# Products of the identity ahead of TensorE's waits in two mixtures' fronts and experts' beginnings

## The chip, the core and the metric

The kernel runs on one core of one Trainium2 chip. The time is that of one execution in microseconds, the median of several runs. The core's engines work side by side and wait for one another by semaphores: TensorE (PE, matrix products), VectorE (DVE), ScalarE (ACT), GpSimd (POOL) and SyncE (SP, which issues DMAs).

## What is computed

Two layers over x of 2 x 1024 tokens by 256, each an attention over a context of 77 rows and a mixture of 8 experts of which every token takes two. The change touches the two mixtures. Cut to them:

```python
def _L0_ffn_ref(hidden_states, router_weight, router_bias, gate_up_proj, gate_up_bias, down_proj, down_bias):
    flat = hidden_states.reshape(B * S, H)
    logits = flat @ router_weight.T + router_bias
    scores = jax.nn.softmax(logits, axis=-1)
    topk_w, topk_idx = jax.lax.top_k(scores, TOP_K)
    gu = jnp.einsum('th,ehn->ten', flat, gate_up_proj) + gate_up_bias
    ...
    down = jnp.einsum('tei,eih->teh', act, down_proj) + down_bias
    gathered = jnp.take_along_axis(down, topk_idx[:, :, None], axis=1)
    out = (gathered * topk_w[:, :, None]).sum(axis=1)

x = x + _L0_xattn_ref(_layernorm(x, axis=-1), ctx_1024, ctx_1024, ...)
x = x + _L0_ffn_ref(_layernorm(x, axis=-1), ...)
x = x + _L1_xattn_ref(ctx_1024, _layernorm(x, axis=-1), ...)
x = x + _L1_ffn_ref(_layernorm(x, axis=-1), ...)
```

The second mixture also normalises the two gates and drops what an expert's capacity doesn't hold. Its hidden width is 1024, the first one's 512.

## The kernel before

The program is a row of blocks. At the end of each, all engines meet, the block's semaphores are cleared, and all go on together. In time: layer 0's attention (to 250 us), mixture 0 (`front` "m0r" from 252, `experts` "m0e" from 290), layer 1's attention (from 525), mixture 1 ("m1r" from 1714, "m1e" from 1752). Each engine runs its own list of instructions in the order written.

**Front** (`front`, line 879). The 2048 tokens are 16 tiles of 128. VectorE normalises a tile (L839, in groups of four), TensorE turns it by two transposes (L956) into one of four PSUM banks, ScalarE copies it out (L988, `xnT`), and TensorE multiplies it with the router (`logits_of`, L947: 128 x 8 columns per product), two tiles behind the transposes. Of each group of four VectorE chooses two experts per token (`choose`, L1011 to L1023); its order is: normalise groups 0 and 1, choose 0, normalise 2, choose 1, normalise 3, choose 2, choose 3. TensorE then waits for all masks (`masks_done`), counts by five bf16 products (L967, L969, `counts_at` lies in the bank of `turned[0]`), and waits for `hot_done`: VectorE meanwhile works out each token's slot by a long chain of small operations and builds one-hot rows in two halves (L1079 to L1083). 16 bf16 products on each half (L974, into `pinv`) invert the list; VectorE turns them into the lists to gather and scatter by (L1092 to L1096). SyncE meanwhile loads up weights, stores the normalised tiles to `xn_rows`, loads the last up weights and a part of the down weights.

**Experts** (`experts`, line 1099). The tokens stand in 39 blocks of 128 rows of one expert. GpSimd gathers rows (L1160), TensorE turns them (`turn_x`, L1182, `pxT`), ScalarE copies them (L1220) and copies the expert's up weights (L1225, `w`), TensorE expands (L1198, 16 products into `ph`), turns the next block, and contracts the block before (L1207, down weights, `py`). At step 1 TensorE waits for `down_ready`: all down weights, whose rest SyncE issues only in this block (L1482, L1471), since their place held the normalised rows until then. Its waits at the beginning are thus: gathered rows, the copies of rows and weights, and, once, the down weights.

fp32 products stand in the trace as two MATMULs each, transposes as one, bf16 products as one.

## Time and profile before

| | us |
|---|---|
| median of 3 runs | 2075.86 (2075.39 to 2076.21) |
| profiled execution | 2081.33 |
| its span | 2079.5 |
| mean granted TensorE clock in it | 0.944 of full |
| TensorE busy | 1897.2 (91%) |
| VectorE busy | 1322.0 (64%) |
| ScalarE busy | 1022.1 (49%) |
| HBM traffic | 50 GB/s over the span |

The profiled execution is 5.5 us above the median. The granted clock is a share of 2.4 GHz, so 0.50 is 1.2 GHz. The page shows it in 40 slices; it is 0.8 or more nearly everywhere, 0.5 in the slices that begin at 260 and 1716 us, and 0.6 and 0.7 in those of 520 and 572. How to read the shares: 91% is a mean of stretches with different limits, and what matters for a change in a front is which wait ends last there.

### The profile page before, as it was taken

How to read it: one execution, taken by the hardware profiler on the slowest of the kernel's cores; microseconds unless marked ns; L12 is line 12 of the kernel's file. 1: busy time of each engine (PE TensorE's matmuls, PEld its weight loads, DVE VectorE, ACT ScalarE, POOL GpSimd, SP SyncE). 2: the span in 40 equal slices, each digit the busy share in tenths (PEclk: the TensorE clock that was granted, in tenths of full speed). 3: DMA queues.
4: the chain of work that ended last, by engine and by line, in shares of the span. 5: the costliest groups of instructions: out<-in, count | busy, mean ns of one | idle time of the engine just before them, and what ended most of it. 6: DMA issues, size and time to landing. Idle time of an engine off the chain costs nothing. (4 is left out here: it accounts for less than half of the span.)

```text
span 2079.5 us, 40140 instructions
## 1 busy us (share of the span) xinstructions
PE 1897.2 (91%) x13658; PEld 1648.1 (79%) x13659; DVE 1322.0 (64%) x2970; ACT 1022.1 (49%) x1761; POOL 608.6 (29%) x542
## 2 busy tenths in 40 slices
PE   6899859999479999999999999999999985999994
PEld 3678759999468888888888888888888865899993
DVE  5445246767657877787787778877777875222223
ACT  3554325554245555555555555555555642444441
POOL 3000003332243432343244324432443200222220
PEclk9999859999679999999999999999999995999997
DMA  6242271111333212320331133213311209111114
GB/s 209 94 145 78 92 285 45 47 48 41 109 72 72 55 39 54 72 53 22 72 72 42 31 73 72 44 32 73 73 35 40 65 2 380 48 36 35 35 35 134
DMA packets 94348, 159.18 MB, mean 77 GB/s; under 512 B 23389, under 2 KB 55513, under 8 KB 92382
## 3 DMA queue, kind: packets, MB, share of 16 engines
q1 hardware_dynamic: 83982, 134.28, 22.7%
q0 software_dynamic: 7888, 20.54, 3.2%
q8 instruction: 101, 1.65, 0.4%
q10 hardware_dynamic: 2304, 2.10, 0.3%
q14 instruction: 73, 0.60, 0.1%
HBM read 71.44 MB, written 32.41 MB: 50 GB/s over the span
## 5 line engine op out<-in xcount | busy, mean ns | idle before, releaser
L1942 ACT ACTIVATE a_prob<-a_slot,a_npeak 128x848 f32<-128x848 f32 x256 | 248.5, 971 | 205.6 <-DVE a_npeak L2003 205.2
L1808 PE MATMUL a_slot<-a_KHL,a_QHL 128*128 128x424 f32 (+1 forms) x1536 | 301.8, 345 | 11.2 <-DVE a_probT L2024 9.3
L2001 DVE TENSOR_REDUCE a_part_peak<-a_slot 128x2 f32<-128x848 f32 x256 | 265.4, 1037 | 37.9 <-PE a_slot L1808 36.8
L1955 ACT ACTIVATE a_probT<-a_slot 128x640 f32<-128x640 f32 x256 | 180.7, 706 | 197.7 <-PE a_slot L1817 153.6
L1833 PE MATMUL a_po<-a_probT,a_V 128*64 128x256 f32 (+1 forms) x2304 | 276.8, 385 | 0.0
L1817 PE MATMUL a_slot<-ident,a_prob 128*128 128x128 f32 x2048 | 268.8, 275 | 0.0
L1808 PEld LDWEIGHTS a_slot<-a_KHL,a_QHL 128*128 128x128 f32 x1536 | 237.9, 191 | 38.5 <-ACT a_probT L1955 13.6
L2033 DVE CUSTOM_DVE_ANT_0 a_masked<-a_prob,a_maskr,a_latent_sum 128x253 f32<-128x253 f32 x256 | 181.8, 710 | 102.5 <-ACT a_prob L1944 87.5
L1817 PEld LDWEIGHTS a_slot<-ident,a_prob 128*128 128x128 f32 x2048 | 236.3, 143 | 8.7 <-issue 0.5
L1833 PEld LDWEIGHTS a_po<-a_probT,a_V 128*64 128x64 f32 (+1 forms) x2304 | 153.8, 136 | 83.3 <-issue 7.3
L1758 PEld LDWEIGHTS a_side<-a_W,a_latT 128*128 128x128 f32 x1536 | 196.6, 199 | 24.1 <-issue 10.8
L1758 PE MATMUL a_side<-a_W,a_latT 128*128 128x128 f32 x1536 | 204.9, 285 | 9.9 <-ACT a_latT L1388 3.8
L2024 DVE COPY a_probT<-a_slot 128x512 f32<-128x512 f32 x256 | 175.2, 685 | 5.2 <-PE a_slot L1817 4.5
L1198 PEld LDWEIGHTS m1e_ph<-m1e_xT,m1e_w 128*128 128x128 f32 x1248 | 147.3, 194 | 8.0 <-ACT m1e_w L1225 3.1
L1198 PE MATMUL m1e_ph<-m1e_xT,m1e_w 128*128 128x128 f32 x1248 | 147.8, 277 | 5.5 <-DMA m_down<-in_L_ffn_W_dram 2.8
L1198 PEld LDWEIGHTS m0e_ph<-m0e_xT,m0e_w 128*128 128x128 f32 x1248 | 147.7, 194 | 6.0 <-ACT m0e_w L1225 3.3
L1198 PE MATMUL m0e_ph<-m0e_xT,m0e_w 128*128 128x128 f32 x1248 | 148.2, 278 | 3.4 <-ACT m0e_w L1225 2.9
L1207 PE MATMUL m1e_py<-m_down,m1e_h 128*128 x624 | 141.0, 379 | 0.0
L1264 DVE TENSOR_TENSOR m1e_h<-m1e_ph,m_bup 128x1024 f32<-128x1024 f32 x39 | 47.8, 1225 | 132.2 <-PE m1e_ph L1198 132.2
L1698 POOL TENSOR_TENSOR a_square<-a_knat 128x1152 f32<-128x1152 f32 x15 | 32.2, 2144 | 336.2 <-ACT a_V L1927 336.2
L1207 PEld LDWEIGHTS m1e_py<-m_down,m1e_h 128*128 128x128 f32 x624 | 115.6, 190 | 14.2
L1944 ACT ACTIVATE a_prob<-a_slot,a_npeak 128x253 f32<-128x253 f32 x256 | 121.1, 473 | 0.0
(321 smaller groups left out, 3021.7 us busy)
## 6 DMA issues: line engine op xcount, KB each, us to landing
a_KHL<-a_KT SPq DMA_DIRECT2D x128, 256.0 KB, 4.4
a_QHL<-a_QT SPq DMA_DIRECT2D x128, 128.0 KB, 2.4
m_up<-_L_ffn_gate_up_proj_dram SPq DMA_DIRECT2D x8, 1024.0 KB, 9.4
m_up<-in_L_ffn_W_dram SPq DMA_DIRECT2D x8, 1024.0 KB, 8.8
m_down<-in_L_ffn_W_dram SPq DMA_DIRECT2D x8, 1024.0 KB, 11.9
a_prob_dram<-a0p_zeros SPq DMA_DIRECT2D x4, 1632.0 KB, 10.7
a_dist_dram<-a_dist SPq DMA_DIRECT2D x4, 1632.0 KB, 5.3
a_band_prob<-a_prob_dram SPq DMA_DIRECT2D x4, 1632.0 KB, 6.9
```

Source lines behind the costliest of these rows:

```text
L1198: ins = nc.tensor.matmul(ph[:, q, cols], w[:, q, c, cols], xT[:, c, :], start=c == 0, stop=c == EC - 1)
L1207: ins = nc.tensor.matmul(py[1 - q][:, 0:E], a[:, 1 - q, f * P:(f + 1) * P], down[:, bass.ds(e, 1), f, :].rearrange("p a n -> p (a n)"), st ...
L1758: ins = t_.matmul(out, x[:, c, :], W[:, parity, i, c, :], start=c == 0, stop=c == EC - 1)
L1808: ins = t_.matmul(out[:, i * BANK:i * BANK + hi - lo], q, KHL[:, pair.parity, h, part, lo:hi], start=part == 0, stop=part == 1)
L1817: ins = t_.transpose(out[:, j * P:(j + 1) * P], prob[:, u % 2, j * P:(j + 1) * P], ident[:, :])
L1833: ins = t_.matmul(po_t[h * D1:(h + 1) * D1, :], V[0:rows, pair.parity, j, h, :], probT[0:rows, gi % 2, j, h, :], start=j == PARTS[0][0], s ...
L1942: a_.activation(prob[:, u % 2, 0:2 * CUT].rearrange("p (n k) -> p n k", n=2), two_banks(slot[u % 2]), ACT.Exp, bias=bias, accum_out=latent ...
L1944: a_.activation(prob[:, u % 2, 2 * CUT:], slot[u % 2][:, 2 * BANK:2 * BANK + REST], ACT.Exp, bias=bias).then_inc(exped, 1)
L1955: a_.activation(probT[:, u // 4 % 2, HALF:KT_TILES, h, u % 2 * P:(u % 2 + 1) * P], slot[u % 2][:, HALF * P:KT_TILES * P].rearrange("p (t q ...
L2001: v.tensor_reduce(part[:, 0:2], two_banks(slot[u % 2]), AX.X, ALU.max).then_inc(part_peaked, 1)
L2024: v.tensor_copy(probT[:, u // 4 % 2, 0:HALF, h, u % 2 * P:(u % 2 + 1) * P], slot[u % 2][:, 0:HALF * P].rearrange("p (t q) -> p t q", q=P)) ...
L2033: v.tensor_tensor_reduce(masked[:, :], prob[:, u % 2, 2 * CUT:], maskr[:, pair.b, :], 1.0, latent_sum[:, u % 2:u % 2 + 1], ALU.mult, ALU.a ...
```

## The change

`keep_clock(nc, out, ident, n)` makes n products of the identity with itself into a place of PSUM that nobody reads. It is called in TensorE's list alone, and it waits for nothing. In each front: 8 ahead of the loop, 1 ahead of each odd tile from the 3rd index on (7 in all), 6 after the last logits, 20 ahead of the wait for the first half of the one-hot rows, and 6 after the last product on them. In each experts' beginning (step 0 only): 16 ahead of the first `turn_x`, 8 after it. To have a place for them, `pinv` becomes a view of a whole bank (`pinv_bank`); the last six of the front go to the bank of `counts_at`, those of the experts to `ph`.

```diff
+def keep_clock(nc, out, ident, n):
+
+    for _ in range(n):
+        nc.tensor.matmul(out, ident[:, :], ident[:, :], start=True, stop=True)
...
-        pinv = ctx.enter_context(nc.psum_tensor(f"{name}_pinv", [P, 3, BLOCKS], F32))
+        pinv_bank = ctx.enter_context(nc.psum_tensor(f"{name}_pinv", [P, BANK], F32))
+        pinv = pinv_bank[:, 0:3 * BLOCKS].rearrange("p (k b) -> p k b", k=3)
...
+            idle = pinv_bank[:, 0:P]
+            keep_clock(nc, idle, ident, 8)
             for t in range(TILES):
+                if t % 2 and t > 2:
+                    keep_clock(nc, idle, ident, 1)
                 pe.wait_ge(dst_done, t + 1)
...
             logits_of(TILES - 1)
+            keep_clock(nc, idle, ident, 6)
             pe.wait_ge(masks_done, TILES // LN_GROUP)
...
                 if k == 0:
+                    if half == 0:
+                        keep_clock(nc, idle, ident, 20)
                     pe.wait_ge(hot_done, half + 1)
...
             ins.then_inc(inverse_done, 1)
+            keep_clock(nc, counts_at[:, 0:P], ident, 6)
...
                 if isinstance(s, int) and s == 0:
+                    keep_clock(nc, ph[:, 0, 0:P], ident, 16)
                     turn_x(0, 0)
+                    keep_clock(nc, ph[:, 0, 0:P], ident, 8)
```

TensorE's list at the start of mixture 0's front, before (L956 transposes, L947 logits; x counts products or transposes of the program):

```order
L67 UNCONDITIONAL_BRANCH
L938 UNCONDITIONAL_BRANCH
L956 MATMUL m0r_turned<-ident,m_down 128x128 x6
L947 MATMUL m0r_pl<-router_Wr,a_latT 128x8 x2
L956 MATMUL m0r_turned<-ident,m_down 128x128 x2
```

The same place now (L845 the added products, L968 transposes, L954 logits):

```order
L945 UNCONDITIONAL_BRANCH
L845 MATMUL m0r_pinv<-ident 128x128 x8
L968 MATMUL m0r_turned<-ident,m_down 128x128 x6
L954 MATMUL m0r_pl<-router_Wr,a_latT 128x8 x2
L845 MATMUL m0r_pinv<-ident 128x128
```

Eight products stand ahead of the first transposes, and then one ahead of every second tile.

TensorE's list from the last logits of the front into the experts, before (L967 and L969 counts, L974 the inversion, L1182 turned rows, L1198 expansion):

```order
L947 MATMUL m0r_pl<-router_Wr,a_latT 128x8 x6
L967 MATMUL m0r_turned<-m0w_M,m0r_ones 128x256
...
L969 MATMUL m0r_pp<-m0w_M,m0r_earlier 128x256
L974 MATMUL m0r_pinv<-m0r_blk1h,m_bdown 128x117 x32
...
L1182 MATMUL m0e_pxT<-ident,m0e_xg 128x128 x2
L1198 MATMUL m0e_ph<-m0e_xT,m0e_w 128x128 x16
```

The same place now:

```order
L845 MATMUL m0r_pinv<-ident 128x128 x6
...
L982 MATMUL m0r_pp<-m0w_M,m0r_earlier 128x256
L845 MATMUL m0r_pinv<-ident 128x128 x20
L989 MATMUL m0r_pinv<-m0r_blk1h,m_bdown 128x117 x32
L845 MATMUL m0r_turned<-ident 128x128 x6
...
L845 MATMUL m0e_ph<-ident 128x128 x16
L1198 MATMUL m0e_pxT<-ident,m0e_xg 128x128 x2
L845 MATMUL m0e_ph<-ident 128x128 x8
L1216 MATMUL m0e_ph<-m0e_xT,m0e_w 128x128 x16
```

Nothing else has moved on TensorE, and the lists of the other engines are the same but for line numbers. Mixture 1 reads alike.

## Rows read from the trace of the kernel before

**Rows 1.** Table of stretches (us, busy per engine, PEclk, DMA share, GB/s)

```profile
255.00:272.00 17.00, 17.00 (x87) 16.93 (x86) 7.84 (x58) 7.26 (x18) 0.00 (x0) 0.50 1.02 397
272.00:283.00 11.00, 1.24 (x6) 0.58 (x5) 9.61 (x40) 0.41 (x2) 0.00 (x0) 0.50 1.05 378
...
300.94:305.80 4.86, 4.86 (x23) 4.86 (x24) 0.00 (x0) 1.75 (x1) 0.00 (x0) 0.50 0.73 257
305.90:307.90 2.00, 1.44 (x13) 1.23 (x13) 0.63 (x1) 0.51 (x2) 0.00 (x0) 1.00 0.00 0
...
1762.61:1766.70 4.09, 4.09 (x19) 4.09 (x20) 0.00 (x0) 1.74 (x1) 0.00 (x0) 0.50 1.08 387
1766.80:1771.40 4.60, 1.84 (x17) 1.61 (x15) 1.22 (x1) 2.69 (x4) 0.00 (x0) 1.00 0.72 256
```

**Rows 2.** TensorE's timeline, mixture 0 (start us, us, what, [idle before, releaser])

```profile
252.76 1.54 PE L956 MATMUL m0r_turned<-ident,m_down 128*128 128x128 f32 x6 [5.74 <-DVE m_down L839]
...
269.46 2.57 PE L947 MATMUL m0r_pl<-router_Wr,a_latT 128*128 128x8 f32 x12
273.87 1.00 PE L967 MATMUL m0r_turned<-m0w_M,m0r_ones 128*128 128x256 bf16 x4 [1.84 <-DVE m0w_M L1023]
...
283.42 1.80 PE L974 MATMUL m0r_pinv<-m0r_blk1h,m_bdown 128*128 128x117 bf16 x16 [8.34 <-DVE m_bdown L1083]
286.41 1.79 PE L974 MATMUL m0r_pinv<-m0r_blk1h,m_bdown 128*128 128x117 bf16 x16 [1.19 <-DVE m_bdown L1083]
297.37 0.69 PE L1182 MATMUL m0e_pxT<-ident,m0e_xg 128*128 128x128 f32 x2 [9.17 <-DMA m0e_xg<-m_xn_rows,m_gather]
300.94 6.18 PE L1198 MATMUL m0e_ph<-m0e_xT,m0e_w 128*128 128x128 f32 x32 [2.88 <-ACT m0e_w L1225]
306.96 0.38 PE L1182 MATMUL m0e_pxT<-ident,m0e_xg 128*128 128x128 f32 x2
```

**Rows 3.** VectorE's timeline, front of mixture 0 and the next block's start

```profile
252.29 2.67 DVE L839 TENSOR_SCALAR m_down<-xres,m0n_moments,m0n_rstd 128x256 f32<-128x256 f32 x8 [3.20 <-PEq L67]
...
258.64 0.19 DVE L1011 TENSOR_TENSOR m0r_logits<-m0r_pl,router_br 128x32 f32<-128x32 f32 x1 [3.22 <-PE m0r_pl L947]
...
260.30 1.38 DVE L839 TENSOR_SCALAR m_down<-xres,m0n_moments,m0n_rstd 128x256 f32<-128x256 f32 x4
263.32 0.19 DVE L1011 TENSOR_TENSOR m0r_logits<-m0r_pl,router_br 128x32 f32<-128x32 f32 x1 [1.64 <-PE m0r_pl L947]
...
272.07 0.19 DVE L1011 TENSOR_TENSOR m0r_logits<-m0r_pl,router_br 128x32 f32<-128x32 f32 x1 [2.30 <-PE m0r_pl L947]
...
288.24 0.20 DVE L1092 COPY m0r_low<-m0r_pinv 128x39 f32<-128x39 f32 x1 [0.77 <-PE m0r_pinv L974]
...
290.25 0.20 DVE L859 TENSOR_TENSOR m0w_free<-m0w_free,m0w_unused 128x39 f32<-128x39 f32 x1 [1.02 <-PEq L67]
```

**Rows 4.** Chain of work that ended last, mixture 1 (start us, us, what)

```profile
1758.81 12.60 DMA m_down<-in_L_ffn_W_dram
...
1778.96 3.57 PE m1e_ph L1198 x32
```

**Rows 5.** TensorE's timeline near the kernel's start, transposes and the next products

```profile
15.51 3.68 PE L154 MATMUL a0ln_turned<-ident,a0p_xn 128*128 128x128 f32 x16 [1.11 <-DVE a0p_xn L134]
20.40 1.29 PE L336 MATMUL a_pk<-a0p_ctxT,a0p_Wk 128*128 128x154 f32 x8 [1.22 <-PEq L67]
```

**Rows 6.** Table of stretches, end of layer 0's attention, columns as in rows 1

```profile
193.00:196.60 3.60, 1.88 (x18) 1.81 (x17) 1.61 (x7) 2.10 (x3) 1.01 (x1) 1.00 0.02 5
196.70:200.00 3.30, 3.30 (x16) 3.12 (x16) 0.00 (x0) 0.98 (x2) 0.00 (x0) 0.50 0.00 0
...
224.00:227.30 3.30, 1.67 (x11) 1.34 (x11) 1.83 (x6) 1.15 (x2) 0.00 (x0) 1.00 0.00 0
...
247.90:252.20 4.30, 0.00 (x0) 0.00 (x0) 1.16 (x7) 0.00 (x0) 1.01 (x1) 0.50 0.00 0
```

**Rows 7.** TensorE's timeline, second expansion of mixture 1

```profile
1771.45 3.84 PE L1198 MATMUL m1e_ph<-m1e_xT,m1e_w 128*128 128x128 f32 x32 [2.81 <-DMA m_down<-in_L_ffn_W_dram]
```

## The prediction

> **What bounds the kernel now.** I read the table of stretches first, since the change lives in four short places of a 2079.5 us span. In the front of mixture 0 TensorE is busy without a break from 255 to 272 us, and the granted clock is 0.50 all that time, as it is after it (272 to 283) and in the experts' first expansion from 300.94 [rows 1]. The front of mixture 1 reads the same. So some 55 us per mixture run at 1.2 GHz instead of 2.4. The TensorE timeline then shows which of that is TensorE's own time: the loop of transposes and logits (252.76 to 272.03), a wait of 1.84 us for the masks, one of 8.34 us for the one-hot rows, 16 + 16 bf16 products with 1.19 us between them, a wait of 9.17 us for the gathered rows, one of 2.88 us for the weights' copy, and 32 expansions in 6.18 us [rows 2]. The VectorE timeline shows who is waited for. VectorE waits for logits at 258.64 (3.22 us), 263.32 (1.64 us) and 272.07 (2.30 us), so TensorE sets the loop; from 272 to 288 VectorE's own chain sets the time, and it waits only 0.77 us for the last bf16 product [rows 3]. Last, the chain of waits: in mixture 1 the second expansion, at 1771.45, is released by a load of the down weights that took 12.60 us to land [rows 4], and the DMA engines are saturated on the way there (1.08 of their time from 1762.61 to 1766.70) [rows 1]. In mixture 0 they are at 0.73 in the stretch that ends at 305.8 and at 0.00 after it [rows 1].
>
> **What one added product costs.** A product of the identity by itself is 128 columns of fp32, as one expansion product, and fp32 expansions stand as two MATMULs in the trace (16 in the order, x32 in the trace). At the high clock 32 of these take 3.57 us [rows 4], or 0.11 each, so 0.22 for a product. At the low clock 16 transposes of 128 columns took 3.68 us [rows 5], 0.23 each, so 0.45 for a product. There are 8 + 7 + 6 + 20 + 6 = 47 in each front and 24 in each experts' beginning.
>
> **Front, the eight ahead.** TensorE enters the block with the others, about when VectorE's first normalisation starts (252.29) [rows 3]. Eight at the low clock are 3.6 us, to 255.85; the first transpose ran at 252.76 [rows 2]. Cost 3.1 us, on the path, since TensorE sets the loop. They can't run at the high clock: TensorE has been idle for 5.7 us by then, and the clock fell within that idle [rows 2, 6].
>
> **When the clock comes up.** In the expansion at 300.94 it was still 0.50 at 305.8 and is 1.00 right after; in that of 1762.61 it is 0.50 to 1766.7 and 1.00 from 1766.8 [rows 1]. So it rose 4.9 and 4.2 us after dense work began. From 252.25 that gives about 256.8: one microsecond into the loop.
>
> **Whether it stays up.** This decides the case. At the high clock a tile of the loop (two transposes, four logit MATMULs) takes about 0.59 us instead of 1.17. But then TensorE runs out of tiles: the third and fourth groups are normalised only after VectorE has chosen for the groups before. The three starts 258.64, 263.32 and 272.07 [rows 3] are 4.68 us apart per group; by my reckoning of the choice (1.7, from 258.64 to the next normalisation at 260.30), normalisation (0.75 to the second tile), two tiles of TensorE and one single product (1.0), latencies (0.3), a group takes 3.7 us at the high clock. In it TensorE streams 8 transposes and 2 products: 8 x 0.11 + 2 x 0.22, about 1.3 us of 3.7, as the logit MATMULs have 8 columns. Nearest rows: the stretch 224.0 to 227.3 has 1.67 us busy of 3.30 and keeps 1.00; that of 193.0 to 196.6 has 1.88 of 3.60, a good part of it in MATMULs of 34 and 51 columns, and the next stretch is at 0.50 [rows 6]. [...] I take it that the clock rises, holds while the first eight tiles are there for the taking, and is lost again when TensorE starts to wait for VectorE.
>
> A rule weighed here: the Trainium skill, "TensorE: Matmul & The Clock Gate", Part 4 (PE-mode transpose), says that the full clock does not engage in transpose mode. This trace speaks against it: after 3.68 us of transposes alone the next product, of 154 columns, ran 8 MATMULs in 1.29 us [rows 5], which is the high pace. By the page the loop would have to live on its single products and the clock would surely be lost; by the row the transposes count, and the case in which it holds keeps a chance.
>
> **The front's sum, clock lost.** Eight ahead: -3.1. Seven singles, five at the low clock (0.45) and two at the high (0.22): -2.7. Some seven tiles at 0.59 instead of 1.17: +4.1. Six after the logits: 2.7 us at the low clock in a wait of 1.84 [rows 2]: -0.9. Twenty: at most 8.9 us in a wait of 8.34, less once the clock rises: 0. Second half of the bf16 products: 1.79 us would be 0.9, and VectorE's wait of 0.77 [rows 3] is all there is to gain; the clock may be either: +0.4. Six at the end: VectorE has 1.0 us left after 288.24 before both meet at the block's end (its idle of 1.02 before 290.25) [rows 3]; they take 1.3 to 2.7: -0.3 to -1.7, taken as -0.6. Sum -2.8 us (the front ends later).
>
> **Experts of mixture 0.** Sixteen (3.6 to 7.2 us) lie in the 7.1 us from the block's start at 290.25 to the gathered rows at 297.37: hidden. Eight (1.8 to 3.6) lie in 2.88 us plus the tail of the transposes: hidden at the high clock. Then the first expansion runs warm: to the next transposes at 306.96 it took 6.02 us, it would take 3.57: +2.45, and the two transposes before it, 0.69, some +0.3. Next in line is the wait for the down weights before the second expansion. DMA is quiet by 305.8 [rows 1]; at -2.8 from the front it is no obstacle. Sum for mixture 0: -2.8 + 2.75, about 0.
>
> **Mixture 1.** The front ends 2.8 us later here too, the first expansion starts at 1765.4 and takes 3.6: 1769.0, with transposes and their copy 1769.9. The down weights come at 1771.45 [rows 4]. Their DMA is issued 2.8 us later, but the engines have a backlog (their share is full, 1.05 in the same place of mixture 0 and 1.08 here [rows 1]), so I leave them there: 0, with a bound of 1 us against. The first expansion's end has 2.81 us of slack today [rows 7]: neither a faster front nor a faster first expansion can gain here. That caps the whole change. Everything after 1771.45, and both long stretches of experts and attention, have the same instructions at a clock of 1.00.
>
> **Forecast.** 2081.33 us of the profiled execution (2079.5 span and 1.8 around it) stand 5.5 above the median of 2075.86; the sum of about 0 applies to both: 2075.9. Own range 2073.5 to 2078.5, from the ends of the last six (1.1), the tiles at the high clock (+/- 2 tiles, 1.2) and 1 us in mixture 1.
>
> **Rivals.**
> 1. The clock holds through the loop. For it: transposes count, and 224 to 227.3 held with half its time idle. Then each front: the first choice starts 1 us late, three group gaps (4.7, 4.7, 4.0) shrink by 1.0, 1.0 and 1.6, so +2.6; the singles are in that; the first six are hidden (1.3 in 1.84); then +0.4 and -1.4, as after twenty products (4.5 of 8.34 us) TensorE idles long enough to lose the clock for the last six: +1.5. Mixture 0: 1.5 + 2.75 = +4.2. In mixture 1 the first expansion would end at about 1764.7, and TensorE would idle 6 us until the down weights; an idle of 5.7 us lost the clock at 252 [rows 6], one of 2.81 kept it [rows 1, 7]. The second expansion then starts low and gives back up to 2.45, say 2.0. Total +2.2: 2073.7; without that loss 2071.7.
> 2. The clock never comes up in the loop (the change doesn't do what it says). The 17 us of unbroken work at 0.50 [rows 1] show that the loop itself doesn't raise it; if eight products are too short a start, the loop runs low with all additions on top: 3.1 + 3.1 + 0.9 + 0.6 + 1.7 = 9.4 per front. Mixture 0: 9.4 - 2.75 = 6.7. Mixture 1: the second expansion at 1762.61 + 9.4 + 3.6 + 0.9 = 1776.5, 5.1 after the down weights. Total 11.8 slower: 2087.7. It turns slower by over 0.2% from some 3 us more than the 2.8 forecast per front, and mixture 1 starts to lose from 4.3 us of delay on. Against it: 3.6 us of products and three tiles' transposes without a gap come close to the 4.2 and 4.9 us after which it rose.
> 3. The forecast with a warm first expansion followed by a lost clock in mixture 1: 2 us more, 2078. It needs TensorE to idle about 4 us or more before 1771.45, so a front that ends no later than now.
>
> **How the numbers follow.** Forecast 0.55, holds 0.27, never comes up 0.08, rival 3 0.10. Measurement tells 0.2% from no change, 4.15 us. Faster: of the holding case the part near 2071.7, and a little for sizes, 0.17. Slower: rival 2 and the upper part of rival 3, 0.12. Within: 0.71. Range 2072.0 to 2079.5, which leaves out rival 2 and the best end of rival 1.
>
> **What would show it.** Right: the clock column reads 0.50, then 1.00 for some 5 to 10 us from about 257, then 0.50 before 272; the third group's choice starts within 1.5 us of today's; the first expansion of both mixtures takes about 3.7 us; the second expansion of mixture 1 is still released by the down weights. Wrong, on the fast side: 1.00 up to the masks and a front shorter by 1.5 us or more; or down weights that land earlier in mixture 1, which I exclude because DMA is saturated. Wrong, on the slow side: 0.50 throughout the loop, or a second expansion of mixture 1 of 5 to 6 us.

## The result, and the profile after

The changed kernel took 2090.86 us in the median of 10 runs (2084.83 to 2099.02), the kernel before 2076.03 in the median of 10 runs beside it (2069.35 to 2084.02). The ratio is 1.0063, with a 95% interval of 1.0046 to 1.0080. That is slower by 13 us, outside the range of 2072.0 to 2079.5 and on the side that had a chance of 0.12.

The traced execution took 2095.3 us, with a span of 2093.5 against 2079.5. Its mean granted clock is **higher** than before, 0.952 against 0.944, and TensorE is busy 40 us longer. Both come with the added products, and neither is time saved. The head of the page after, with the clock row in 40 slices:

```profile
span 2093.5 us, 40708 instructions
...
PE 1937.2 (93%) x13942; PEld 1687.0 (81%) x13943; DVE 1321.6 (63%) x2970; ACT 1021.5 (49%) x1761; POOL 608.3 (29%) x542
...
PEclk9999879999679999999999999999999997999997
```

I cut both traces at four places: SyncE's first DMA issue of a front (the entry), its first issue of the experts (`m_bdown`; from entry to here is "the front"), the start of the second expansion, and its end. All times in us; the start and the end of the second expansion are counted from the entry:

| kernel | mixture | entry | front | 2nd expansion starts | it takes | it ends |
|---|---|---|---|---|---|---|
| before | 0 | 252.24 | 37.96 | 55.66 | 3.81 | 59.47 |
| before | 1 | 1714.18 | 37.97 | 57.27 | 3.84 | 61.11 |
| after | 0 | 256.04 | 41.64 | 57.83 | 3.81 | 61.64 |
| after | 1 | 1721.46 | 42.23 | 61.94 | 5.87 | 67.81 |

The 14.0 us between the two spans are then 3.8 before the first entry, 2.2 in mixture 0, 1.3 from there to mixture 1, and 6.7 in mixture 1. After that both take 304.2. The first and third of these lie in stretches whose instructions are the same, and they are taken up last.

**Front of mixture 0, after.** The TensorE timeline (start, length, engine, line, operation, output<-inputs, count; in brackets the idle time before and who ended it), against [rows 2]. L845 are the added products:

```profile
256.09 3.75 PE L845 MATMUL m0r_pinv<-ident 128*128 128x128 f32 x16 [5.27 <-PEq L67]
259.63 1.49 PE L968 MATMUL m0r_turned<-ident,m_down 128*128 128x128 f32 x6
260.91 0.91 PE L954 MATMUL m0r_pl<-router_Wr,a_latT 128*128 128x8 f32 x4
261.68 0.58 PE L845 MATMUL m0r_pinv<-ident 128*128 128x128 f32 x2
...
277.89 2.91 PE L845 MATMUL m0r_pinv<-ident 128*128 128x128 f32 x12
...
281.62 5.01 PE L845 MATMUL m0r_pinv<-ident 128*128 128x128 f32 x40
290.18 1.80 PE L989 MATMUL m0r_pinv<-m0r_blk1h,m_bdown 128*128 128x117 bf16 x16 [3.55 <-DVE m_bdown L1099]
293.18 1.80 PE L989 MATMUL m0r_pinv<-m0r_blk1h,m_bdown 128*128 128x117 bf16 x16 [1.19 <-DVE m_bdown L1099]
294.77 2.18 PE L845 MATMUL m0r_turned<-ident 128*128 128x128 f32 x12
```

The stretches of the same front (busy time of PE, weight loads, DVE, ACT, POOL; granted clock; DMA share; GB/s), against [rows 1]:

```profile
260.00:262.00 2.00, 2.00 (x12) 1.92 (x11) 0.00 (x0) 1.15 (x3) 0.00 (x0) 0.52 1.02 416
262.00:264.00 2.00, 2.00 (x21) 2.00 (x20) 0.00 (x0) 0.97 (x3) 0.00 (x0) 1.00 1.03 422
264.00:266.00 2.00, 1.84 (x17) 1.75 (x17) 1.42 (x15) 1.98 (x6) 0.00 (x0) 1.00 1.02 412
266.00:268.00 2.00, 1.43 (x14) 1.43 (x15) 1.49 (x5) 1.46 (x4) 0.00 (x0) 1.00 1.06 416
268.00:270.00 2.00, 2.00 (x16) 2.00 (x15) 1.58 (x16) 0.77 (x3) 0.00 (x0) 0.69 1.02 399
270.00:272.00 2.00, 2.00 (x11) 2.00 (x12) 1.32 (x5) 0.70 (x2) 0.00 (x0) 0.50 1.02 403
```

The clock comes up at 261.9, 5.8 us after the eight began, and is lost near 268.8. Against [rows 3], VectorE's choices for the four groups start here:

```profile
264.45 0.19 DVE L1027 TENSOR_TENSOR m0r_logits<-m0r_pl,router_br 128x32 f32<-128x32 f32 x1 [5.22 <-PE m0r_pl L954]
268.28 0.19 DVE L1027 TENSOR_TENSOR m0r_logits<-m0r_pl,router_br 128x32 f32<-128x32 f32 x1 [0.80 <-PE m0r_pl L954]
273.49 0.19 DVE L1027 TENSOR_TENSOR m0r_logits<-m0r_pl,router_br 128x32 f32<-128x32 f32 x1 [2.17 <-PE m0r_pl L954]
278.08 0.19 DVE L1027 TENSOR_TENSOR m0r_logits<-m0r_pl,router_br 128x32 f32<-128x32 f32 x1 [2.84 <-PE m0r_pl L954]
...
297.73 0.20 DVE L865 TENSOR_TENSOR m0w_free<-m0w_free,m0w_unused 128x39 f32<-128x39 f32 x1 [1.73 <-PEq L67]
```

From the entry that is 8.41, 12.24, 17.45 and 22.04, where before had 6.40, 11.08, 15.77 and 19.83. The one gap at the high clock is 3.83; the others are 5.21 and 4.59, longer than before's 4.69 and 4.06.

**Mixture 1, after.** TensorE's second expansion and, below it, the stretches around the block's end at 1763.7. The row of before that answers is [rows 7], with 3.84 us and 2.81 idle:

```profile
1777.48 0.38 PE L1198 MATMUL m1e_pxT<-ident,m1e_xg 128*128 128x128 f32 x2
1783.40 5.87 PE L1216 MATMUL m1e_ph<-m1e_xT,m1e_w 128*128 128x128 f32 x32 [5.53 <-DMA m_down<-in_L_ffn_W_dram]
```

```profile
1758.00:1760.00 2.00, 1.51 (x16) 1.51 (x17) 1.49 (x4) 0.00 (x0) 0.00 (x0) 0.50 1.09 386
1760.00:1762.00 2.00, 2.00 (x12) 2.00 (x11) 0.89 (x5) 0.00 (x0) 0.00 (x0) 0.50 0.56 197
1762.00:1764.00 2.00, 1.22 (x6) 0.95 (x6) 0.26 (x2) 0.00 (x0) 0.00 (x0) 0.50 0.00 0
1764.00:1766.00 2.00, 2.00 (x10) 2.00 (x10) 1.85 (x9) 0.00 (x0) 1.29 (x2) 0.50 0.69 188
```

SyncE's list in the same place (SPq: its issues; the second row is its first issue in the experts):

```profile
1743.91 10.36 SPq L1489 DMA_DIRECT2D m_down<-in_L_ffn_W_dram  x4
1763.69 0.34 SPq L1500 DMA_DIRECT2D m_bdown<-in_L_ffn_b_dram  x1
1764.09 9.77 SPq L1489 DMA_DIRECT2D m_down<-in_L_ffn_W_dram  x4
```

The DMA engines ran dry: their share is 0.56, then 0.00 for the 2 us before 1764. In before they were at work up to the experts' first issue at 1752.15 and beyond it:

```profile
1750.00:1752.00 2.00, 0.16 (x2) 0.00 (x0) 0.89 (x5) 0.00 (x0) 0.00 (x0) 0.50 1.09 385
1752.00:1754.00 2.00, 0.00 (x0) 0.00 (x0) 1.70 (x8) 0.00 (x0) 1.07 (x1) 0.50 1.11 390
```

The later end of the front was therefore passed on to the down weights, which arrived after the first expansion and its transposes had left TensorE idle for 5.53 us. In that idle the clock fell, and the second expansion took 5.87: the clock was at 1.00 up to 59.4 us after the entry and again from 66.2 us on, and the expansion ran from 61.94 to 67.81.

### The profile page after: what moved, and what is told of

Its sections match the earlier page's. It is cut to its first block and busy times, and to the rows that moved or that the text cites. A ratio compares the mean times of both kernels' runs of the same rounds, so it can differ in the third digit from the quotient of the medians.

```text
span 2093.5 us, 40708 instructions
## 1 busy us (share of the span) xinstructions
PE 1937.2 (93%) x13942; PEld 1687.0 (81%) x13943; DVE 1321.6 (63%) x2970; ACT 1021.5 (49%) x1761; POOL 608.3 (29%) x542
```

## The experiments

All edits are against the changed kernel; times of mixture stages are from each one's trace. Kernels in one paragraph's table ran beside before on the same chip.

### One part at a time

`e1_experts_only` takes the five calls out of `front` and keeps the 16 and 8 of the experts:

```diff
-            keep_clock(nc, idle, ident, 8)
...
-                if t % 2 and t > 2:
-                    keep_clock(nc, idle, ident, 1)
...
-            keep_clock(nc, idle, ident, 6)
...
-                    if half == 0:
-                        keep_clock(nc, idle, ident, 20)
...
-            keep_clock(nc, counts_at[:, 0:P], ident, 6)
```

> Only the products of the experts' beginning (16 and 8) are kept, all 47 of each front are left out. From the front's first DMA issue to the first DMA issue of the experts it is 37.97 us before and 41.6 (mixture 0) and 42.2 (mixture 1) with the whole change. Theory A (the cost sits in the longer front and, in mixture 1, in DMA engines that run dry and in a second expansion at the low clock): 38.0 in both mixtures here; mixture 0's second expansion starts 53.0 to 53.6 after the front's first issue instead of 55.66, as the first one runs at the high clock; mixture 1's starts at 57.3 as before, but at the low clock, 5 to 6 us instead of 3.84. In time about -0.5 to the kernel before: 2075.5. Rival B (the products cost something everywhere, in proportion to their number, 48 of 142): +5 us, 2081.

`e2_front_only` is the reverse:

```diff
-                    keep_clock(nc, ph[:, 0, 0:P], ident, 16)
                     turn_x(0, 0)
-                    keep_clock(nc, ph[:, 0, 0:P], ident, 8)
```

> Only the 47 products of each front are kept, the 24 of each experts' beginning are left out. Theory A: fronts of 41.6 and 42.2 us as with the whole change; mixture 0's second expansion 59.3 to 59.8 after the front's first issue (55.66 before, 57.8 with the whole change), since the first one now runs low; mixture 1's second expansion starts at 61.9 as with the whole change, for the down weights, and takes 3.8, as the first one, low and late, leaves TensorE too short an idle to lose the clock. Time +8.5: 2084.5. Rival B: +10 us spread over the kernel, mixture 1's second expansion anywhere.

`e3_no_loop` takes the eight ahead and the singles out:

```diff
-            keep_clock(nc, idle, ident, 8)
...
-                if t % 2 and t > 2:
-                    keep_clock(nc, idle, ident, 1)
```

> The whole change without the eight ahead of the loop and the seven singles. Theory A: the loop is as before (last choice 19.8 us after the front's first issue, 22.0 with the whole change), the six after it cost 0.7, the last six 0.7, so the front takes 39.4 to 39.6; mixture 0's second expansion at 54.4; mixture 1's down weights within 1 us of 57.3, the second expansion low (5 to 6 us). Time +1.3: 2077.3. If the eight and the singles were not what makes the fronts long, these stay near 42 and the time near 2090.

`e4_loop_only` keeps these two and takes all others out:

```diff
-            keep_clock(nc, idle, ident, 6)
...
-                    if half == 0:
-                        keep_clock(nc, idle, ident, 20)
...
-            keep_clock(nc, counts_at[:, 0:P], ident, 6)
...
-                    keep_clock(nc, ph[:, 0, 0:P], ident, 16)
...
-                    keep_clock(nc, ph[:, 0, 0:P], ident, 8)
```

> Only the eight ahead of the loop and the seven singles. Theory A: fronts of 40.2 us (+2.2), the clock up for 7 to 10 us in the loop and then lost; mixture 0's second expansion at 57.9; mixture 1's down weights 1 to 2 us later than 57.3, the second expansion at the high clock, 3.8 us. Time +3.5: 2079.5. If the clock holds here, the front comes below 38.

Beside them before took 2079.86 us. "Stages" is the end of the second expansion from the entry, mixture 0 and 1, against before's 59.47 and 61.11.

| kernel | median | ratio to before (95%) | front 0, 1 | last choice 0, 1 | stages 0, 1 |
|---|---|---|---|---|---|
| e1_experts_only | 2076.47 | 0.9973 (0.9957 to 0.9989) | 37.97, 37.97 | as before | -2.2, +1.7 |
| e2_front_only | 2087.9 | 1.0036 (1.0022 to 1.0051) | 46.73, 41.81 | 26.52, 22.15 | +7.8, +4.8 |
| e3_no_loop | 2079.87 | 1.0000 (0.9981 to 1.0018) | 39.79, 40.06 | as before | +1.1, +4.7 |
| e4_loop_only | 2083.28 | 1.0020 (0.9997 to 1.0042) | 40.77, 40.34 | 22.62, 22.21 | +1.7, +5.3 |

What follows. By the ratios, the experts' part alone is a small gain and the front's part a loss; a cost of the products wherever they stand, the other theory put up for e1 (+5 us), is excluded. In the front, the loop's products cost 2.8 and 2.4 us (e4), and those behind the loop 1.8 and 2.1 (e3).

The ratios and the stages don't agree in size. The two stages together say -0.5 us for e1, +12.6 for e2, +5.8 for e3 and +7.0 for e4; the ratios say -5.6, +7.5, 0 and +4.2. So of e1's gain the stages show 0.5 us. The difference lies outside them: in these four traces the unchanged way from mixture 0 to mixture 1 took 1393.0 to 1396.8 us, against 1402.5 in the trace of before. That spread is taken up last.

Mixture 1 loses in all four, since none brings the down weights earlier. In e4 it also lost the clock, which was not expected: its first expansion ran low (6.79 us), and the second took 5.32 after an idle time of 2.92. In e1 the front is as long as before's, the first expansion is 1.98 us shorter, and TensorE waits the rest and falls to the low clock:

```profile
1750.17 3.84 PE L1209 MATMUL m1e_ph<-m1e_xT,m1e_w 128*128 128x128 f32 x32 [0.89 <-ACT m1e_w L1236]
...
1759.33 5.31 PE L1209 MATMUL m1e_ph<-m1e_xT,m1e_w 128*128 128x128 f32 x32 [5.11 <-DMA m_down<-in_L_ffn_W_dram]
```

One front went another way. In mixture 0 of e2 the eight products took as long as in the others (3.75 us from 246.92), but the clock stayed low through the whole loop, the last choice was 6.7 us late, and the front was 8.8 us longer than before's. This is the prediction's rival 2 (9.4 per front), in one front:

```profile
253.00:256.00 3.00, 3.00 (x17) 3.00 (x16) 0.00 (x0) 0.97 (x3) 0.00 (x0) 0.50 1.04 421
256.00:259.00 3.00, 3.00 (x16) 3.00 (x15) 1.50 (x15) 1.80 (x4) 0.00 (x0) 0.50 1.01 403
...
266.00:270.00 4.00, 4.00 (x21) 4.00 (x21) 1.21 (x14) 1.15 (x3) 0.00 (x0) 0.50 1.10 379
```

### Does a longer front reach the down weights?

`e10_end_only` has no added product but 12 at the end of each front, where they do nothing except lengthen it:

```diff
-            keep_clock(nc, counts_at[:, 0:P], ident, 6)
+            keep_clock(nc, counts_at[:, 0:P], ident, 12)
```

> The kernel before with 12 products after the front's last bf16 product and nothing else: it lengthens the front alone, behind all of its work. At the low clock 12 take 5.4 us, of which 1.0 lies beside VectorE: front 42.2 us instead of 37.97. Theory A (mixture 1's down weights come late because the front is longer: the DMA engines run dry before the rest of the loads is issued): mixture 1's second expansion starts at 61.5 to 62 us after the front's first issue, as with the whole change (61.94), with a stretch of 2 to 3 us of idle DMA before the experts' first issue. Rival C (the down weights come late for something else that the products do, such as TensorE's reading beside the DMA's writing in the experts): 57.3 to 58.5, since TensorE makes nothing there.

Mixture 1's front took 40.91, 2.94 longer (42.2 in all was expected; the clock came up within the 12); its second expansion started at 60.30, 3.03 later; one execution took 2093.07. The DMA engines run out in the same way (stretches of e10, whose experts' first issue is at 1764.32; below them TensorE's second expansion):

```profile
1762.00:1764.00 2.00, 1.58 (x13) 1.39 (x11) 0.00 (x0) 0.00 (x0) 0.00 (x0) 0.92 0.58 204
1764.00:1766.00 2.00, 0.00 (x0) 0.00 (x0) 1.53 (x7) 0.00 (x0) 0.98 (x1) 0.93 0.35 123
...
1783.71 3.84 PE L1208 MATMUL m1e_ph<-m1e_xT,m1e_w 128*128 128x128 f32 x32 [2.79 <-DMA m_down<-in_L_ffn_W_dram]
```

So the delay passes one for one. Over all kernels with the loads as they were, the second expansion starts 18.9 to 21.1 us after the experts' first issue: 19.30 to 19.87 in three traces of before, 18.92 to 19.71 in four of the changed kernel, 19.39 in e10. The backlog of DMA was worth less than 2 us: with the issue moved back, the front's own loads are through 39.6 us after the entry (the share of 0.56 in the changed kernel, of 0.58 here), and before issues at 37.97, 1.6 us ahead of that. Even these 1.6 us can't be seen in the landings. e10 makes the delay alone: its second expansion kept the clock.

`e5_early_down` lets SyncE issue all four late loads of down weights in the front, before it waits for the block's end:

```diff
+            sp.wait_ge(logits_done, TILES)
+            load_weights(sp, 2)
...
+                if stage == 2:
+                    load_down(sp, range(NE - lent, NE))
...
-                load_down(sp, range(NE - lent, NE))
```

> The whole change, and the rest of the down weights is loaded in the front, as soon as the normalised rows are stored and the last logits are made (their place is free then), instead of in the experts. The front keeps its length. Theory A: no idle DMA in mixture 1, its second expansion starts at 57.3 to 58.5 after the front's first issue instead of 61.94, still at the low clock; mixture 0's stays at 57.8. Time -4 us to the changed kernel. Rival C: 61 to 62 as before it.

2083.38 us, ratio 1.0018 (1.0002 to 1.0034), beside a before of 2078.66. The second expansion no longer waits for DMA, but mixture 1's front grew to 46.23. SyncE is held by its own issues, and everyone waits for it at the block's end (SyncE, then TensorE, whose idle time now lies there):

```profile
1743.14 22.55 SPq L1491 DMA_DIRECT2D m_down<-in_L_ffn_W_dram  x8
1766.57 1.69 SPq L1504 DMA_DIRECT2D m_bdown<-in_L_ffn_b_dram  x1
...
1766.62 6.54 PE L845 MATMUL m1e_ph<-ident 128*128 128x128 f32 x32 [4.30 <-PEq L67]
...
1781.12 3.81 PE L1218 MATMUL m1e_ph<-m1e_xT,m1e_w 128*128 128x128 f32 x32 [0.56 <-ACT m1e_xT L1240]
```

`e12_two_early` issues two of the four there, in mixture 1 alone:

```diff
+                if stage == 2 and layer == 1:
+                    load_down(sp, range(NE - lent, NE - lent + 2))
...
-                load_down(sp, range(NE - lent, NE))
+                load_down(sp, range(NE - lent + 2 * layer, NE))
```

> The whole change, and in mixture 1 two of the four late down weight loads are issued in the front, once the last logits are made, so that SyncE is done with them at about 39 us, ahead of the front's own end. Theory A: the front stays at 42.2, the DMA engines stay full up to its end, the second expansion of mixture 1 starts at 57.5 to 59.5 instead of 61.94, still low. Rival C: 61 to 62.

2085.14 us, 1.0018 (0.9999 to 1.0036), beside a before of 2078.42. Here SyncE is free in time (front 42.62, against 42.23 in the changed kernel), and the second expansion starts at 57.66 instead of 61.94, released by ScalarE's copy and not by a load, and takes 3.81:

```profile
1743.23 15.84 SPq L1491 DMA_DIRECT2D m_down<-in_L_ffn_W_dram  x6
1763.35 0.34 SPq L1504 DMA_DIRECT2D m_bdown<-in_L_ffn_b_dram  x1
1763.74 3.69 SPq L1491 DMA_DIRECT2D m_down<-in_L_ffn_W_dram  x2
...
1778.39 3.81 PE L1218 MATMUL m1e_ph<-m1e_xT,m1e_w 128*128 128x128 f32 x32 [0.57 <-ACT m1e_xT L1240]
```

That takes 6.3 of mixture 1's 6.7 us away. The late issue of the down weights is the cause of that part, shown from both sides: e10 makes the delay, e12 takes it away and with it the idle time in which the clock fell.

### Keeping the clock in the wait for the down weights

`e6_step1_filled` adds products ahead of that wait in mixture 1:

```diff
+                    keep_clock(nc, ph[:, 1, 0:P], ident, 24 if layer == 1 else 0)
```

> The whole change with 24 products more in mixture 1, between the first expansion and the wait for the down weights (5.53 us of idle in the changed kernel, after which the second expansion took 5.87). 24 at the high clock take 5.35 us. Theory A: the second expansion of mixture 1 starts where it did, at 61.9 after the front's first issue, and takes 3.8 us: -2.0 us there. If the products delay more than they give back, the second expansion starts later than the down weights land and is no longer released by DMA.

The second expansion took 3.84 instead of 5.87, so the low pace came from the idle time. It began at 63.29, not at the 61.9 expected, as the weights landed later in this trace, 21.07 after the first issue; one execution took 2089.79, which says no more than that.

`e8_experts_early_filled` is e1, e5 and e6 together:

> A version meant to beat both: no product in the fronts, 16 and 8 in the experts' beginnings, 24 ahead of the wait for the down weights in mixture 1, and the rest of the down weights loaded in the front. Theory A: fronts of 38.0; mixture 0's second expansion at 53.0 to 53.4 (55.66 before); mixture 1's at 57.3 or a little before, at the high clock, 3.8 us. Sum -2.5 to the kernel before, 0.12%: within what a measurement can tell, so the stages have to show it.

2084.85 us, 1.0024 (1.0009 to 1.0040), beside the same before of 2078.66. Mixture 0 gained 1.9, but SyncE's issues held mixture 1's front to 44.50, as in e5, and the 24 products, with no wait left to fill, stood ahead of the second expansion (63.47). `e11_experts_filled` leaves the loads alone: e1 with 18 products in that wait.

```diff
+                    keep_clock(nc, ph[:, 1, 0:P], ident, 18 if layer == 1 else 0)
```

> A version meant to beat both: nothing in the fronts, 16 and 8 in the experts' beginnings, and 18 products in mixture 1 between the first expansion and the wait for the down weights. Theory A: fronts of 37.97; mixture 0's second expansion at 53.4 after the front's first issue (55.66 before); mixture 1's at 57.3 to 57.5, released by the down weights, and 3.8 us long (5.31 without the 18). Sum -2.2 us to the kernel before, 0.11%, which the stages can show and the times hardly: the ratio should be 0.996 to 1.001.

2074.15 us, 0.9969 (0.9955 to 0.9984) beside a before of 2078.42: 0.3% faster than before, where the changed kernel is 0.6% slower. TensorE in mixture 1 of it:

```profile
1766.02 4.18 PE L845 MATMUL m1e_ph<-ident 128*128 128x128 f32 x36
1771.02 3.84 PE L1210 MATMUL m1e_ph<-m1e_xT,m1e_w 128*128 128x128 f32 x32 [0.82 <-DMA m_down<-in_L_ffn_W_dram]
```

Stages: -2.2 and +0.3. The 18 products are worth 1.4 us in mixture 1 against e1 (+1.7 there); the ratios of the two, 0.9969 and 0.9973, don't tell them apart. Mixture 1 has nothing to gain, as its weights come when they come. That the ratio says some 6 us and the stages say 2 is the same gap as in e1 to e4. Not tried: e12's two early loads with no products in the fronts.

### Can the loop pay if the clock holds?

`e9_more_singles` has 12 products ahead, and one before every tile from the third on:

```diff
-            keep_clock(nc, idle, ident, 8)
+            keep_clock(nc, idle, ident, 12)
...
-                if t % 2 and t > 2:
+                if t > 2:
```

> The whole change with 12 products ahead of the loop instead of 8 and one ahead of every tile from the third index on instead of every second. It asks whether the clock can be held in the loop at all, and what that would be worth. If it holds: the gaps between VectorE's choices are 3.9 to 4.1 us (3.83 where the changed kernel was high, 4.68 before, 5.2 where it had lost the clock), and since 12 products take 4.5 to 5.3 us ahead of it, the last choice comes 20.5 to 21 us after the front's first issue: still later than the 19.83 before. If it doesn't hold: over 23.

The clock held through the loop, in mixture 0 for 27 us:

```profile
260.00:264.00 4.00, 3.87 (x36) 3.83 (x35) 0.40 (x4) 2.44 (x8) 0.00 (x0) 1.00 1.03 417
...
268.00:272.00 4.00, 3.94 (x36) 3.75 (x35) 3.04 (x21) 1.70 (x5) 0.00 (x0) 1.00 1.02 377
272.00:276.00 4.00, 3.60 (x32) 3.39 (x32) 2.87 (x27) 0.56 (x3) 0.00 (x0) 1.00 1.04 366
```

The choices stand at 8.56, 12.40, 16.23 and 18.90 in mixture 0, and the last at 20.06 in mixture 1, against 19.83. The front takes 38.05 and 39.22, against 37.96. So in mixture 0 the loop does gain, 0.93 us (20.5 to 21 was expected), with the clock up 3.1 us after the products began; in mixture 1, where that took 5.5, it loses 0.23. The products behind the loop take back 1.0 in each. Mixture 0's stage is 1.0 us shorter than before's, mixture 1's 3.7 longer. The longer start without the products behind the loop was not run. In mixture 1 the second expansion took 6.20 after 4.92 us idle. One execution took 2086.86.

### Traces of the two kernels again

`e13_change_again` is the changed kernel once more, and so are `e15_change_look` and `e17_change_look_2`; `e14_before_look` and `e16_before_look_2` are the kernel before.

> The changed kernel once more, unaltered, to see which of its stage times repeat. Theory A: fronts between 41.6 and 46.7 by when the clock rises, mixture 1's second expansion 19.4 to 21 after the experts' first issue, and low. The time from the kernel's start to the first front, where no instruction was changed, may differ from 256.04 by several us, as it did between the runs so far (246.9 to 257.2).

> The kernel before, unchanged, for a second trace. The traces so far fall in two kinds in a stretch that no edit touches: from 245 to 255 us after the second expansion of mixture 0 (the beginning of layer 1's attention) the granted clock is 1.00 in five traces and 0.50 in nine, and the stretch from there to mixture 1 takes 1393.0 to 1398.2 us in the first kind and 1402.5 to 1405.8 in the second. The one trace of before is of the second kind. Theory A (the kind falls by chance in every kernel, and so does the 247 to 257 us that it takes to mixture 0): before shows both kinds over its looks, its spread of 2069 to 2084 us being the two kinds. Theory B (before is always of the second kind): 1402 to 1406 us again, 0.50 there.

> The changed kernel, unchanged, third trace. Both traces so far are of the second kind (1403.8 and 1403.9 us, clock 0.50), and entered mixture 0 at 256.0 and 254.0 us. Theory A: it may be of the first kind too. Theory B (the change fixes the kind, by shifting what follows it): 1403 to 1405 us again. In both, the two mixtures read as in the other two traces: second expansion of mixture 1 after an idle time above 4.5 us for the down weights, and 5.3 to 6.2 us long.

> The kernel before once more, third trace, as for e14_before_look. If both looks differ from one another by 7 us in the untouched stretch, the kind falls by chance within one chip; if both are of one kind while the older trace is of the other, it goes with the chip.

> The changed kernel once more, fourth trace. Theory A: the kinds mix as in before. Theory B: 1403 to 1405 us. The changed stages are expected at +2 to +3 us in mixture 0 and +6 to +7 in mixture 1 against before, whatever the kind.

| trace | execution | entry 0 | stages 0, 1 | between | 2nd expansion of mixture 1 |
|---|---|---|---|---|---|
| before | 2081.33 | 252.24 | 59.47, 61.11 | 1402.5 | 3.84 after 2.81 idle |
| e14_before_look | 2081.58 | 255.06 | 59.73, 62.74 | 1398.1 | 5.47 after 2.13 |
| e16_before_look_2 | 2073.88 | 247.75 | 59.39, 61.69 | 1399.1 | 3.84 after 3.27 |
| after | 2095.3 | 256.04 | 61.64, 67.81 | 1403.8 | 5.87 after 5.53 |
| e13_change_again | 2093.5 | 254.03 | 62.05, 67.68 | 1403.9 | 6.06 after 4.54 |
| e15_change_look | 2088.81 | 253.31 | 61.72, 68.13 | 1399.5 | 6.26 after 5.12 |
| e17_change_look_2 | 2093.94 | 254.96 | 62.36, 67.48 | 1403.6 | 6.28 after 3.86 |

The mean stages are 59.5 and 61.8 before, 61.9 and 67.8 after: the changed places cost 2.4 and 5.9 us, 8.3 in all. Each stage repeats within 0.8 us in the changed kernel and within 1.7 in before. The other 5.7 of the 14.0 us between the means of the spans lie in unchanged stretches: entry 2.9, between 2.8. There the two kernels' values overlap.

The unchanged stretches differ by where the granted clock falls. VectorE's list between the mixtures has the same entries in every trace, so it can be cut at the same ones. Of its parts, those in the changed kernel's first trace differ from before's by more than 0.2 us in three: the beginning of layer 1's attention (-0.9, with 61 us at the low clock against 65), and two later ones, +3.9 and -1.5. The +3.9 is this part (before; after; and within it, after):

```profile
795.56:869.82 74.26, 71.66 (x552) 60.33 (x551) 57.86 (x132) 40.94 (x82) 28.39 (x24) 1.00 0.23 52
...
800.57:878.68 78.11, 74.39 (x552) 62.90 (x551) 58.05 (x132) 40.95 (x82) 28.38 (x24) 0.96 0.22 49
811.50:818.30 6.80, 5.98 (x22) 5.58 (x23) 4.18 (x10) 1.26 (x2) 0.00 (x0) 0.50 0.00 1
```

The -1.5 is a part in which before's clock was at 0.50 for 3 us and the changed kernel's wasn't. Before's own three traces differ in the same way: the way between the mixtures took 1398.1, 1399.1 and 1402.5 us with 69, 70 and 77 us at the low clock, and the entry came at 247.75, 252.24 and 255.06 with 15, 25 and 31.

The two theories of the expectations are not settled. All seven traces have the low clock at the beginning of layer 1's attention, but three of them (e14, e15, e16) took 1398.1 to 1399.5 us, below the 1402 that belonged to it there. The fall in the part shown occurs in three of the changed kernel's four traces and in one of before's three (e16), too few to say whether the change moves it.

## Why the prediction was wrong, step by step

**One product's cost**: right, 3.75 us for the eight at the low clock (forecast 3.6).

**When the clock comes up, whether it stays**: the mechanism was right. It rose 5.8 us after the eight began (forecast 4.2 to 4.9), held while tiles were ready, and was lost at about 268.8, when TensorE had begun to wait for VectorE. A group's gap at the high clock is 3.83 (forecast 3.7). The moment is partly luck: over both fronts of the changed kernel's four traces it rose between 3.0 and 5.9 us after the eight began. Two of the signs named for this case were missed narrowly: the third choice is 1.7 us late, not within 1.5, and mixture 0's first expansion took 4.24, not 3.7. The rule of the Trainium skill weighed there, "TensorE: Matmul & The Clock Gate", Part 4, foretold the lost clock too; no run separated transposes from products of few columns, so [rows 5] and the page stand side by side.

**The loop's sum** was -3.1 - 2.7 + 4.1 = -1.7; the last choice is 2.2 us late in both mixtures. The term of seven tiles at the high clock was a little too large. Where the clock rose early and was lost early (mixture 0 of e13 and e17) it is 2.8.

**Behind the loop** the sum was -0.9 + 0 + 0.4 - 0.6 = -1.1; it is -1.5 and -2.1 (front 3.68 and 4.26 longer, less 2.2). Two terms failed. After the twenty, TensorE idles 3.55 and 3.98 us and loses the clock, so both bf16 halves still take 1.80: no gain where +0.4 stood. And the last six then start low: they take 2.18 us in mixture 0, where the clock comes up on the way, and 2.88 in mixture 1, all low. VectorE's wait at the block's end is 1.73 and 2.43 instead of 1.02, so they cost 0.7 and 1.4 where -0.6 stood. I had written that they take 1.3 to 2.7 and taken a value near the cheap end; the idle time ahead of them decided it.

**Experts of mixture 0**: +2.75 forecast. With the front as before (e1) it is 2.2. In the changed kernel it is 1.5: the gathered rows land after 3.99 us of idle, the clock falls once more, and the first expansion takes 4.24 instead of 3.84. So mixture 0 ends 2.2 us later where I wrote "about 0".

**Mixture 1: this is the step that failed.** "Their DMA is issued 2.8 us later, but the engines have a backlog (...), so I leave them there: 0, with a bound of 1 us against." The full share of [rows 1] and the 12.60 us from issue to landing in [rows 4] were read as a queue deep enough to hide the delay. It was less than 2 us deep; the share says how busy the engines are, not how much is queued, and the 1.08 read at 1762.61 is that of the late loads themselves, which a later issue moves along. The front's 4.3 us came through as 4.67 on the second expansion. The bound of 1 us stood where 6.7 were lost. That "neither a faster front nor a faster first expansion can gain here" was right (e1, e11), but that a slower front loses all of its delay was excluded by this reading alone.

**Rival 3** was right in mechanism and size (+2 for the clock lost before the second expansion; measured 5.87 to 6.28 instead of 3.84), and its sign, "a second expansion of mixture 1 of 5 to 6 us", is what came. It was wrong in its condition: I tied it to a front that ends no later than now. The later front moves both the first expansion and the weights, so the idle time grows by what the faster expansion saves, whatever the front does. It belonged in the sum, not beside it with 0.10. With it and the 4.3 of delay, mixture 1 is 6.3 of the 6.7 found.

**Rival 2** occurred in one front of e2 (last choice 6.7 late), not in the changed kernel's own traces. **Rival 1** didn't occur in the change. In e9, where it did with a longer start, the gaps are those that it named (3.84, 3.83 and 2.67), yet the front gains nothing: they pay back the start, and in mixture 0 0.93 us more, which the products behind the loop take.

**What stays open**: 8.3 us are shown in the changed places; the measured difference is 13 us by the ratio. The rest lies in unchanged stretches, where the length goes with where the clock falls; whether the change moves those falls isn't shown. The same gap, with the other sign, stands between ratios and stages in e1 to e4 and e11.

## What to carry to other kernels

Products added to keep the clock pay only in front of work that is bound by TensorE and inside a wait that they don't outlast; price the lead-in at the low clock, and ask of every wait behind them whether it is long enough to lose the clock again. Before a delay is called hidden by a busy transfer queue, look for the end of the busy share against the next issue: if the engines run dry before it, the delay passes one for one. When a stage in front of a fixed arrival gets faster, the time turns into idle, and the work after it can get slower; here 18 more products in that idle, and none in the fronts, gave 0.9969, of which the stages show 2 us of some 6. And when two executions differ outside the changed place, compare the clock there before looking for a cause.

## What the runs showed of the hardware

- **The same eight products don't always raise the clock.** 3.75 us of them at the loop's start were followed by 1.00 from 5.8 us on in the changed kernel, and by 0.50 for another 26 us of unbroken work in e2's mixture 0. In e13's and e17's mixture 0 the clock was up after 3.0 us.
- **No single idle time divides a kept clock from a lost one.** In the kernel before, the second expansion of mixture 1 took 5.47 after an idle time of 2.13 us (e14) and 3.84 after one of 3.27 (e16); in e4 it took 5.32 after 2.92. In e14 and e4 the first expansion had run low almost to its end, 6.40 and 6.79 us, against 5.76 in e16.
- **Executions of the same instructions differ by where the clock falls.** From 245 to 250 us after the end of mixture 0's second expansion, at the beginning of layer 1's attention, the granted clock was 1.00 in five of 18 traces (e1, e2, e3, e4, e8) and 0.50 in the other 13. The way from mixture 0 to mixture 1 took 1393.0 to 1398.2 us in those five and 1398.1 to 1405.8 in the rest, with the same instructions. In before's three traces 8 us more at the low clock went with 4.4 us more of time. This and the entry (246.9 to 257.2) are of the size of the spread in time of one kernel (2069 to 2086 us for before), and one trace of each kernel can't tell 10 us apart; stages measured from their own entry can.
- **SyncE is held by its issues.** Eight loads issued in a row took 22.55 us of its time (e5), six 15.84 (e12), and the block's end waited for it in the first.
